# Attention on one core: VectorE squares two units with one instruction, and ScalarE squares units 5, 6 and 12

## The reference, cut to what matters

```
scores = einsum('bhqd,bhkd->bhqk', q, k) * hs ** (-0.5)
p = softplus(scores)
p = p * p
p = p * causal
attn = p / (sum(p, axis=-1, keepdims=True) + 1e-09)
out = einsum('bhqk,bhkd->bhqd', attn, v)
```

## Time and profile before

| | us |
|---|---|
| median of three runs | 1607.56 (1599.33 to 1610.26) |
| profiled execution, its own time | 1605.87 |
| its span | 1604.0 |
| PE busy | 1520.9 (95%) |
| DVE busy | 1216.4 (76%) |
| ACT busy | 873.0 (54%) |
| POOL busy | 411.4 (26%) |

### The profile page before, as it was taken

How to read it: one execution, slowest core, us unless ns; L and a number is a source line. 1 busy time by engine, 2 the same in 40 slices (tenths; PEclk the granted TensorE clock), 3 DMA queues, 4 the chain that set the end, 5 groups by cost and what they waited for, 6 DMA issues and landing times. The chain is left out here.

```text
span 1604.0 us, 28965 instructions
## 1 busy us (share of the span) xinstructions
PE 1520.9 (95%) x11188; PEld 1125.0 (70%) x11188; DVE 1216.4 (76%) x2334; ACT 873.0 (54%) x1372; POOL 411.4 (26%) x382
## 2 busy tenths in 40 slices
PE   8999898999999998999989999979999999899998
PEld 7888776444444446888867778756777777678777
DVE  4554797898999986664578888768777777688886
ACT  3333387988888886332332222278888887321220
POOL 0002111222122224100433221113555555211111
PEclk9999999999999999999999999999999999999999
DMA  4000065777777750000100000022333333100000
GB/s 159 26 1 14 20 188 178 100 95 106 106 101 102 100 72 2 14 1 1 40 27 8 1 1 1 1 69 78 102 101 107 106 107 107 40 14 27 14 27 27
DMA packets 57160, 95.83 MB, mean 60 GB/s; under 512 B 7904, under 2 KB 29632, under 8 KB 57024
## 3 DMA queue, kind: packets, MB, share of 16 engines
q1 hardware_dynamic: 56064, 93.38, 26.4%
q10 hardware_dynamic: 960, 0.59, 0.1%
HBM read 76.91 MB, written 17.04 MB: 59 GB/s over the span
## 5 line engine op out<-in xcount | busy, mean ns | idle before, releaser
L1438 DVE TENSOR_TENSOR att_weights<-att_weights 128x1024 f32<-128x1024 f32 (+1 forms) x224 | 267.7, 1241 | 39.4 <-ACT att_weights L1411 39.1
L928 DVE SCALAR_TENSOR_TENSOR X<-ps,moe_gsel,X 128x256 f32<-128x256 f32 x512 | 246.1, 483 | 63.5 <-PE ps L48 41.1
L1411 ACT ACTIVATE att_weights<-ps 128x1024 f32<-128x1024 f32 (+1 forms) x288 | 264.9, 992 | 39.8 <-PE ps L1347 20.5
L48 PE MATMUL ps<-w_experts_hi,moe_xh 128*128 128x512 f32 x512 | 205.1, 401 | 1.1 <-DVE X L928 1.1
L48 PE MATMUL ps<-w_experts_hi,moe_xl 128*128 128x512 f32 x512 | 203.3, 397 | 0.0
L48 PE MATMUL ps<-w_experts_lo,moe_xh 128*128 128x512 f32 x512 | 201.6, 394 | 0.0
L1367 PE MATMUL ps<-att_weights,att_v_ones 64*32 64x64 f32 (+5 forms) x2048 | 157.6, 400 | 0.0
L424 ACT ACTIVATE ffn_gates<-ps,ffn_gate_bias 128x512 f32<-128x512 f32 x72 | 49.5, 688 | 148.3 <-PE ps L48 126.6
L48 PEld LDWEIGHTS ps<-w_experts_hi,moe_xh 128*128 128x128 f32 x512 | 96.2, 188 | 27.9 <-DVE X L928 4.5
L48 PEld LDWEIGHTS ps<-w_experts_lo,moe_xh 128*128 128x128 f32 x512 | 96.1, 188 | 22.1
L48 PEld LDWEIGHTS ps<-w_experts_hi,moe_xl 128*128 128x128 f32 x512 | 96.3, 188 | 20.3
(11 more groups left out here) (281 smaller groups left out, 3672.1 us busy)
## 6 DMA issues: line engine op xcount, KB each, us to landing
ssm_lb<-decays SPq DMA_DIRECT2D x32, 512.0 KB, 4.7
ssm_rise<-decays SPq DMA_DIRECT2D x28, 512.0 KB, 3.9
qk_parts<-qkv_part SPq DMA_DIRECT2D x32, 384.0 KB, 2.8
q_stack<-qk_parts SPq DMA_DIRECT2D x64, 128.0 KB, 4.6
k_stack<-qk_parts SPq DMA_DIRECT2D x64, 128.0 KB, 7.8
att_q_stack<-qk_parts SPq DMA_DIRECT2D x64, 128.0 KB, 4.8
att_k_stack<-qk_parts SPq DMA_DIRECT2D x64, 128.0 KB, 8.8
out<-X SPq DMA_DIRECT2D x7, 512.0 KB, 2.9
```

The source lines that it names most:

```text
L48: ins = pe.matmul(out, l(k), r(k), start=first and n == 0, stop=last and n == len(passes) - 1)
L928: dve.scalar_tensor_tensor(out=x, in0=ring[:, e // 2, (e % 2) * C:(e % 2 + 1) * C], scalar=gsel[:, s, j, e:e + 1], in1=x, op0=ALU.mult, op ...
L1411: act.activation(Wt[:, u % WU, 0:n], scores(u)[:, 0:n], ACT.Softplus).then_inc(p_done, 1)
L1438: dve.tensor_tensor(wt, wt, wt, ALU.mult).then_inc(sq_done["dve"], 1)
```

## The change

The table of squarers becomes (5, 6, 12) for ACT; POOL keeps 11. DVE is left with the pairs (0,1), (2,3), (7,8), (9,10), (13,14), (15,16) and the single units 4 and 17. The two places of a pair lie side by side in `att_weights`, so DVE squares each pair with one instruction of 2048 columns, issued at the place in its queue of the pair's second unit, after its softplus. The counts on which PE waits follow.

```diff
-    BY_ACT, BY_POOL = (6, 9, 14), (11,)
+    BY_ACT, BY_POOL = (5, 6, 12), (11,)
     squarer = ["act" if u % PU in BY_ACT else "pool" if u % PU in BY_POOL else "dve" for u in range(NU)]
+    wide = [squarer[u] == "dve" and u + 1 < NU and squarer[u + 1] == "dve" and step_of[u] == step_of[u + 1] and u % WU != WU - 1
+            for u in range(NU)]
+    in_wide = [wide[u] or u > 0 and wide[u - 1] for u in range(NU)]
+    finishes = [not wide[u] for u in range(NU)]
 
     def squares(by, i, u):
 
-        return i * squarer.count(by) + squarer[:u + 1].count(by)
+        done = [x for x in range(NU) if squarer[x] == by and finishes[x]]
+        return i * len(done) + sum(x <= u + wide[u] for x in done)
...
             def square(i, u):
                 dve.wait_ge(p_done, SU + i * NU + u + 1)
-                wt = Wt[:, u % WU, 0:BANKS[u % PU]]
+                wt = Wt[:, u % WU - 1:u % WU + 1] if in_wide[u] else Wt[:, u % WU, 0:BANKS[u % PU]]
                 dve.tensor_tensor(wt, wt, wt, ALU.mult).then_inc(sq_done["dve"], 1)
...
             def body(i, first=False, last=False):
                 for u in range(NU):
-                    if squarer[u] == "dve":
+                    if squarer[u] == "dve" and finishes[u]:
                         square(i, u)
```

## The result

The changed kernel takes 1665.79 us (median of four runs, 1661.36 to 1670.98), the kernel before 1606.22 beside it. The ratio is 1.0377, with an interval of 1.0322 to 1.0431: slower by 3.8%. The forecast was 1674, with a range of 1626 to 1690. The profiled execution of after took 1670.98, with a span of 1669.1, 65.1 more than the span before.

The account below looks back on a forecast made before the run. The prediction took a ring of ACT's and PE's arcs to bound the attention pass, with DVE off it. It summed 1605.87 + 50.4 for late turns + 17.4 for the clock = 1673.7, left at 1674 us; range 1626 to 1690.

Parts of the forecast that it names:

- The ring: Loop of waits that sets each attention pass, 21.27 us: ACT's arc of softplus and squares, then PE's arc.
- The late turn: PE's turn in each pass waits for DVE's copy to att_oT: 3.15 us later, 16 passes, 50.4 us.
- The width: DVE's wide squares replace 96 instructions and free 0.07 us each, 7 us beside the ring: worth nothing on the path.
- two terms of 1.06 and 1.07 us: Added DVE time of the two wider squares ahead of the copy, within the later turn.
- 1.63 us of stand: DVE's square of (9,10) stands 1.63 us a pass while POOL squares unit 11.
- Rival (a): DVE's square of (9,10) starts ahead of POOL's; the turn is 1.52 us late, time 1630 us; chance 0.20.
- The clock: PE's granted clock falls after two of three gaps ahead of the turn, 1.63 us each: 17.4 us, bounds 0 and 26.1.
- ACT's arc: ACT's stretch from the softplus of 5 to that of 11 keeps its length: nothing gained or lost.
- Rival (b): Room hidden in PE's unbroken arc, over 1.5 us, takes up the turn's delay: time 1606 us; chance 0.08.

Follow-up runs that it names:

- the copy first: Changed kernel with the copy to att_oT one place earlier in DVE's queue, ahead of the square of (9,10): 1603.22 us, ratio 0.9994.
- width alone: Changed kernel with the old table put back (ACT squares 6, 9 and 14), so 64 wide squares: 1605.84 us, ratio 0.9999.
- the fastest kernel: Changed kernel with the copy moved earlier and ACT squaring 6, 12 and 14: 1592.34 us, ratio 0.9929; with narrow squares 1593.61 us, 0.9930.
- POOL behind DVE: Changed kernel with one more wait, so POOL squares unit 11 only after DVE has squared (9,10): 1624.57 us, ratio 1.0124.
- PE at work: Changed kernel with PE making the scores of unit 14 five times over, ahead of the turn: 1649.04 us, ratio 1.0282.
- the table alone: Kernel before with the new table (5, 6, 12) and squares of one unit each: 1640.22 us, ratio 1.0224.

## Why the prediction was right

**The ring and the turn.** The late turn was the forecast's main step and holds in size: 3.13 us behind its old place against 3.15, from a softplus of 8 that is 0.94 later (0.92 forecast), a pair that holds DVE 2.21, a division part of 0.83, and a square of (9,10) that holds it 3.78 (3.83). That it is the copy, and nothing else, is shown by the run with the copy first: one place in DVE's queue gives all of it back.

**The width.** The forecast gave it 7 us beside the ring, worth nothing, and two terms of 1.06 and 1.07 us against it in the way to the copy. Both fit: width alone gives 0.9999, and in the fastest kernel 0.9929 stands against 0.9930, while with the new table the wide squares make the turn 1.06 us later than the narrow ones (3.13 against 2.07), and the kernel 1665.79 where it was 1640.22.

**POOL.** The forecast's 1.63 us of stand a pass is shown by the run with POOL behind DVE: the gap falls from 3.06 to 1.49, 1.57 less. The margin by which POOL came first was 0.18, forecast 0.12. Rival (a), DVE in front, came to be in the first pass alone; made to in all, it gave 1624.57 where the rival said 1630. Which of the two engines would be first hung on 0.12 us, with steps good to about 0.1: that the side was right is in part luck, and the forecast gave the other 0.20. The Trainium skill ("SBUF — State Buffer", Who interferes with whom) has it that whichever instruction starts first keeps the shared pair of ports to its end; the runs agree in both directions, with the 3.86 of DVE behind POOL and the 2.21 of POOL behind DVE. The stand of DVE ends some 0.14 ahead of POOL's profiled end.

**The clock.** The mechanism was right, and in the trace the size was short. The forecast took two falls in three passes at 1.63, 17.4 us. In the trace twelve of fifteen passes were longer, by 23.4 us or 1.95 each: in five of them the clock was low for 6.8 us and not 3.4, and it cost 2.6. By medians, against the kernel with PE at work, it is 16.8; the profiled execution is the slowest of the four runs (1661.36 to 1670.98). The mean granted clock of each run agrees with that: 0.973 and 0.975 in the two runs over 1670, 0.978 and 0.980 in the two of 1661, 0.990 to 0.992 in those with PE at work. So the runs of one kernel differ in how long the clock is low, and that the 17.4 lies so near 16.8 is in part luck.

**The rest.** Sixteen late turns were counted; it is fifteen and a small one, since the first pass has no block to divide. The sum of 1674 lies 3 us over the profiled execution, 1670.98, and three differences nearly cancel in it: the late turns gave 46.9 and not 50.4, the 4.8 us of occasional stands came into the base and not into the result, and the clock took 6.0 more. The prediction read from the kernel before that a delay of PE is never given back; in the changed kernel the gap ahead of the turn gives it back, as with POOL behind DVE. The median, 1665.79, lies a further 5.2 under that execution. ACT's arc kept its length, as forecast; 0.31 of wait has moved to the scores of unit 12. Rival (b), room in PE that the profile hides, was refuted for 1.5 us, but it has a grain in it (below).

By the ratios of POOL behind DVE (1.0124), of PE at work in the gap (1.0282) and of the changed kernel (1.0377), the 3.8% are: DVE's longer way to the copy 1.2%, POOL's square across it 1.6% more, the clock 1.0% more.

## What to carry to other kernels

When three engines are each nearly full, find the ring that sets the period and then, for each engine off it, what it owes the ring first; here that was one copy of 0.68 us, with 1.58 us of slack. A small operation that the bounding engine waits for belongs ahead of large ones that nobody waits for yet. Joining two instructions into one saved only what the queue paid between them, here 0.07 us a pair (2.21 against 2.28), and it makes everything behind it wait for the later input and the longer run.

## What the runs showed of the hardware that was not expected

- The clock fell in or right behind twelve of the fifteen gaps of 2.5 to 3.07 us on PE. With the table alone it did so at six of the fourteen gaps of 2.00 us, and with POOL behind DVE at none of 1.49 us. Extra matmuls in the gap made the kernel 16.8 us faster.
- With ACT's arc shorter the pass fell by 0.80 us, to 20.47, where PE's gap before was only 0.63. In a window of one whole pass PE is busy 20.64 us before (399.20 to 420.47) and 20.25 here (394.12 to 414.58), for the same work. So 0.39 us of what the profile shows as busy PE was room. Where it lies is not settled.
- POOL's copies behind its square took 2.67 us and then 0.40, where they took 1.61 and 1.28. The first ran beside DVE's long square; most of the second ran while DVE was idle (445.81 to 447.02). That the square held the first one up fits this, but no run tests it.
